# Matrix products between blocks of attention scores, as pairs of 64-row tiles, with a new order on all engines

## What is computed

```python
# one layer; layer 0 also normalizes q and k per head (_ln over the 18 numbers of a head, gains g_q, g_k)
mod = silu(c) @ w_mod + b_mod                       # six vectors of 288 per sample
xn  = _ln(x) * (1 + scale_msa) + shift_msa
q, k, v = split_heads(xn @ w_qkv + b_qkv)           # 16 heads of 18
attn = softmax(einsum('bhqd,bhkd->bhqk', q, k) * 18 ** -0.5)
x = x + gate_msa * (merge_heads(attn @ v) @ w_proj + b_proj)
xn2 = _ln(x) * (1 + scale_mlp) + shift_mlp
x = x + gate_mlp * (gelu(xn2 @ w1 + b1) @ w2 + b2)  # 288 -> 1152 -> 288
```

## Time and profile before

| what | value |
|---|---|
| time, median of 3 runs | 2550.83 us (2548.33 to 2554.66) |
| profiled execution, its span | 2554.1 us |
| PE busy | 2371.3 us (93%), 21219 matmuls |
| PEld busy | 1990.4 us (78%) |
| DVE busy | 1852.2 us (73%) |
| ACT busy | 1626.7 us (64%) |
| POOL busy | 714.5 us (28%) |
| chain that ended last | PE 63%, DVE 11%, DMA 8% |

### The profile page before, as it was taken

How to read it: one execution, slowest core, us unless ns; L and a number is a source line. 1 busy time by engine, 2 the same in 40 slices (tenths; PEclk the granted TensorE clock), 3 DMA queues, 4 the chain that set the end, 5 groups by cost and what they waited for, 6 DMA issues and landing times.

```text
span 2554.1 us, 56620 instructions
## 1 busy us (share of the span) xinstructions
PE 2371.3 (93%) x21219; PEld 1990.4 (78%) x21219; DVE 1852.2 (73%) x3456; ACT 1626.7 (64%) x3049; POOL 714.5 (28%) x938
## 2 busy tenths in 40 slices
PE   5558999999999999999999899999999999999998
PEld 3336878878888888888787788888888888888878
DVE  6357787787788777777677777777777777777764
ACT  3256666676666766767666666666676666666653
POOL 2012332332333233333222122223222222223222
PEclk8788999999999999999999999999999999999999
DMA  4776757756666666666846755566556655565531
GB/s 102 131 174 106 121 116 121 122 112 119 116 118 115 116 120 112 117 118 112 148 85 111 145 97 100 97 113 103 99 99 105 110 96 104 100 113 97 98 67 42
DMA packets 259208, 280.91 MB, mean 110 GB/s; under 512 B 25930, under 2 KB 243212, under 8 KB 258936
## 3 DMA queue, kind: packets, MB, share of 16 engines
q1 hardware_dynamic: 243888, 247.40, 55.8%
q10 hardware_dynamic: 15048, 29.89, 4.5%
HBM read 101.86 MB, written 26.73 MB: 50 GB/s over the span
## 4 chain that ended last, share of the span: by engine, by line
PE 63%; DVE 11%; DMA 8%; issue 5%; SPq 5%; ACT 4%; POOL 3%; DVEq 0%; POOLq 0%; ACTq 0%
PE psum L783 13%; PE psum L873 7%; PE psum_exp L783 7%; PE psum_max L783 7%; DMA attn_k_stack<-attn_qk_hi 5%; PE psum L933 5%; PE psum L935 5%; PE psum L934 5%; PE psum_exp L849 5%; DVE attn_maxima L1105 4%; PE psum_max L862 4%; SPq L1364 4%; DVE attn_qk_centred L1143 3%; PE psum L790 2%; ACT attn_probs L969 1%
## 5 line engine op out<-in xcount | busy, mean ns | idle before, releaser
L969 ACT ACTIVATE attn_probs<-psum_exp 128x1024 f32<-128x1024 f32 x512 | 526.9, 1029 | 391.4 <-PE psum_exp L849 377.6
L1105 DVE TENSOR_REDUCE attn_maxima<-psum_max 128x4 f32<-128x1024 f32 x512 | 620.6, 1212 | 83.0 <-PE psum_max L862 77.4
L1278 POOL TENSOR_TENSOR mlp_x<-mlp_x,mlp_gated 128x288 f32<-128x288 f32 x128 | 103.4, 808 | 1035.4 <-DVE mlp_gated L1122 1035.4
L783 PE MATMUL psum<-attn_ln_split,w_qkv_split 128*128 128x256 f32 (+3 forms) x2240 | 339.2, 297 | 5.1 <-DVE attn_neg_max_lo L1132 3.1
L933 PE MATMUL psum<-mlp_w_fc_hi,mlp_hidden_hi 128*128 128x288 f32 x1152 | 340.9, 296 | 2.9 <-DVE mlp_w_fc_lo L770 2.0
L934 PE MATMUL psum<-mlp_w_fc_lo,mlp_hidden_hi 128*128 128x288 f32 x1152 | 340.5, 296 | 0.0
L935 PE MATMUL psum<-mlp_w_fc_hi,mlp_hidden_lo 128*128 128x288 f32 x1152 | 340.2, 295 | 0.0
L783 PEld LDWEIGHTS psum<-attn_ln_split,w_qkv_split 128*128 128x128 f32 (+3 forms) x2240 | 284.2, 183 | 54.3 <-issue 25.8
L862 PE MATMUL psum_max<-attn_k_stack,attn_q_stack 62*128 62x256 f32 x2048 | 221.1, 294 | 103.6 <-DMA attn_k_stack<-attn_qk_hi 56.0
L873 PE MATMUL psum<-attn_probs,attn_v 128*32 128x256 f32 x4096 | 282.6, 394 | 1.1 <-ACT attn_probs L969 1.1
L849 PE MATMUL psum_exp<-attn_q_stack,attn_k_stack 64*128 64x256 f32 x2048 | 260.5, 332 | 20.9 <-ACT attn_probs L969 10.9
(11 more groups left out here) (170 smaller groups left out, 4222.1 us busy)
## 6 DMA issues: line engine op xcount, KB each, us to landing
attn_q_stack<-attn_qk_hi SPq DMA_DIRECT2D x256, 128.0 KB
attn_k_stack<-attn_qk_hi SPq DMA_DIRECT2D x256, 128.0 KB
attn_o_and_sums<-attn_o_transposed SPq DMA_DIRECT2D x256, 128.0 KB, 5.0
mlp_gate_and_gated_bias<-modulation ACTq DMA_DIRECT2D x64, 288.0 KB, 3.9
attn_qk_squares<-qk_rstd SPq DMA_DIRECT2D x32, 512.0 KB
attn_q_stack<-attn_qk_lo SPq DMA_DIRECT2D x128, 128.0 KB
attn_k_stack<-attn_qk_lo SPq DMA_DIRECT2D x128, 128.0 KB
attn_x<-in_x_dram SPq DMA_DIRECT2D x32, 288.0 KB, 7.6
```

What stands on the lines that cost most here:

```text
L783: mm = q.matmul(to, lhs, rhs, start=(i == 0), stop=(i == 6))
L969: q.activation(probs[r][:], ps_exp[:], ACT.Exp, scale=SCORE_SCALE).then_inc(S["exps"], 1)
L1105: q.tensor_reduce(maxes[g % 2][:, p // QUARTER, :, p % QUARTER, :], ps_max[:].rearrange("p a (t n) -> p a t n", t=TT), AX.X, ALU.max).then ...
L1278: q.tensor_tensor(xt, xt, gated2[:], ALU.add).then_inc(S["added2"], 1)
```

## The change

Three things change together.

First, the products of v, the projection, the MLP and four of the query and key chunks are made two outputs at a time. A pair of outputs (`low`, `high`) goes into two banks. In a first pass one uses the lower 64 rows of each operand and the other the upper 64 rows, as two tiles of 64 rows at once; in a second pass they change places. A wait for the first pass stands ahead of the second, since both write the same bank. Where no block of scores stands between the two passes (`spaced` is false), the products stay whole, 128 rows each.

```diff
+        def lower_and_upper(q, low, high, half, split):
+            for i in range(len(WIDE_PAIRS) if split else 0):
+                done_low = part_matmul(q, low, i, LOWER, i == 0, False)
+                done_high = part_matmul(q, high, i, UPPER, i == 0, False)
+            if split:
+                done_low.then_inc(S[half], 1)
+                done_high.then_inc(S[half], 1)
+                halves[half] = halves.get(half, 0) + 2
+        def upper_and_lower(q, low, high, split):
+            for i in range(len(WIDE_PAIRS)):
+                first, last = not split and i == 0, i == len(WIDE_PAIRS) - 1
+                done_low = part_matmul(q, low, i, UPPER if split else ROWS, first, last)
+                done_high = part_matmul(q, high, i, LOWER if split else ROWS, first, last)
+            return done_low, done_high
...
+                if (g := due(T, V_FIRST)) is not None:
...
+                    lower_and_upper(q, *[v_product(g, t) for t in range(TT)], "v_half", spaced(T, when(V_SECOND, g)))
+                if (g := due(T, V_SECOND)) is not None:
+                    split = spaced(when(V_FIRST, g), T)
+                    if split:
+                        q.wait_ge(S["v_half"], halves["v_half"])
+                    low, high = upper_and_lower(q, *[v_product(g, t) for t in range(TT)], split)
```

```diff
-                    for m in range(CHUNKS):
-                        j, half = divmod(m, 2)
-                        if half == 0:
-                            bank = bank_of(("fc1", g, j))
-                        mm = wide_matmul(q, bank[:, half * N:half * N + N], w1, slice(m * P, m * P + P), acts2, slice(0, N), True)
+                    for m in (0, 4):
+                        products = [fc1_product(g, m + i) for i in range(4)]
...
+                        lower_and_upper(q, products[0], products[1], "fc1_half", True)
...
+                        lower_and_upper(q, products[2], products[3], "fc1_half", True)
+                        for i, pair in enumerate((products[0:2], products[2:4])):
+                            q.wait_ge(S["fc1_half"], CHUNKS // 2 * 2 * g + m + 2 * i + 2)
+                            low, high = upper_and_lower(q, *pair, True)
```

Third, the table of places is new for all engines. Places are now in quarters of a slot (STEP = 4), a step's read-out has a place of its own on each engine, and a dict gives single samples (the first ones, those around the boundary of the layers, the last one) places of their own. Banks are written out in tables instead of being picked. One line of the table before, and what answers to it:

```diff
-VAR_AT = -28
-RSTD_OUT, RSTD_IN = -26, -25
+VAR_AT, RS_AT = (-28.25, -28.25, {B - 1: -29.0}), (-28.25, -28.25, {0: -31.5, B - 1: -29.0})
+RSTD_OUT, RSTD_IN = -28.25, -23.25
```

374 lines of the change are left out of this document (231 added, 143 removed).

## The result

The changed kernel takes 2542.52 us, median of 6 runs (2530.15 to 2544.57), against 2551.26 us before (6 runs, 2548.33 to 2554.66): ratio 0.9954, 95% interval 0.9942 to 0.9966. It is faster, by 9 us where the forecast said 121. Its profiled execution spans 2540.5 us, 13.6 less than before.

The account below looks back on a forecast made before the run. PE's own queue was taken to bound the steady part. The sum 2554.1 - 73 + 10 - 25 - 25 - 10 = 2431 put the median at about 2430 us, with 50% on 2400 to 2465 and a wider range of 2380 to 2500.

Parts of the forecast that it names:

- Pairs at the pace of whole products: PE's products: a pair of 64-row products costs the 0.12 us of one full product, so taken at nothing.
- rival 4: PE's pairs don't keep the scores' pace; above 0.1335 us a pair all gains go, at 0.15 2700 us; chance 6%.
- Changes of shape: PE's tile shape changes fall from 1448 to 1048, at 0.19 or 0.11 us each: -73 us.
- Second halves wait: On PE, second halves wait for first halves' semaphore where only one block of scores lies between: +10 us, 0 to +20.
- Scores spread out: PE's steady waits, 63 us, shrink by 40% as score blocks for the maxima stand further apart: -25 us, 0 to -60.
- First samples: At the start, the landing of the keys' stack falls out of the loop of three samples: -25 us, 0 to -45.
- The boundary: Around the change of layers, own places for the samples there give back PE's idle time: -10 us, 0 to -15.
- rival 2: DVE's in-order queue keeps layer 0 near 37.7 us a sample, only layer 1 gets shorter: median about 2505; chance 7%.
- Rival 1: The order removes no wait; only the 73 us of shape changes come, less 10 for half waits: median 2488; chance 20%.

Follow-up runs that it names:

- the first experiment: Changed kernel's order of all engines, but with whole 128-row products in place of the pairs of half products: 2605.97 us, ratio 1.0194 to the kernel before.
- e14: Changed kernel with the eight chunks of the MLP's first product as whole products one after the other, the rest in pairs: 2555.16 us, ratio 1.0002.
- e2: Changed kernel with layer 1's PSUM banks for the value products and the last two query and key chunks dealt out anew: 2591.01 us, ratio 1.0141.
- e3: Changed kernel with layer 1's first transpose of the maxima one block of scores later on PE: 2541.04 us, ratio 0.9938.
- e4: Changed kernel with the banks of the MLP's first four products swapped, chunks 0 and 1 with 2 and 3: 2561.59 us, ratio 1.0032.
- e12: Changed kernel with the loads of layer 0's MLP weights 4 and 7 slots later on ScalarE's queue: 2540.11 us, ratio 0.9933.
- e16: Changed kernel with layer 1's last MLP chunk in bank 7 and the transposes' second bank 6, exchanging the two: 2537.32 us, ratio 0.9937.
- e18: e16 plus, in layer 1, projection's second halves behind the third probability product (so far 2572.74 us), and first query and key pair later: 2593.62 us, ratio 1.015.

## Why the prediction was wrong

*Pairs at the pace of whole products:* right, 0.120 and 0.132 us; rival 4 never had a case here. The code's DMA grew to 244 packets in 0.8% of the engines' time, and in the steady stretches PE's waits without a named releaser are none in ten samples of layer 0 and 0.8 us in ten of layer 1. The Trainium skill, "TensorEngine Tiling (Array Packing)", section Instruction Overhead, puts about 60 cycles of overhead on each matmul; this trace does not bear that out as a cost to be added: with 9118 more matmuls a pair keeps the 0.120 and 0.132 us of a whole product.

*Changes of shape, -73 us:* right on PE: 1.17 and 1.22 us a sample, and -74 by the same steps over the whole program. *Second halves wait, +10:* right in kind and size. The semaphore itself costs 0.01 us, but the load behind it is uncovered, 0.1 us, at one or two places a sample. It is contained in the waits below.

***Scores spread out, -25:* this is the step that failed.** It took 40% of the 63 us of steady waits away; they grew instead, by 1.08 us a sample in layer 0 and 0.97 in layer 1, +50 us over the 52 samples of the parts above. I had followed one kind of wait, the scores' blocks for the reductions, and it did get better: in layer 1 the one of up to 0.6 us before the maxima is gone. I had not gone along the other round trips in the new order: which bank each product takes and who empties it. Before, banks were dealt to whichever had been free longest; now they are fixed, pairs need two at once, and bank 4 is asked for right behind the probability product that fills it. With whole tiles this makes the order's waits equal to before's; that the rest, 0.9 to 1.2 us, comes with the pairs is shown by the first experiment. For three places of layer 1 the traces show how (a change of shape stood over a round trip, and taking it away bought waiting); with two first loads of second halves they make up 0.77 of 0.91 us. For layer 0 the trace names the waits (the keys' stack, which was not among PE's waits in ten samples before, and the maxima) and the chain through the reciprocals' transfers, 12 us long in the sample shown; that this chain makes the added wait is argued and not shown. I had costed every change as if it were on the path.

*First samples, -25:* measured -6.7, of which some 3.5 are changes of shape. The variance product did go ahead, but the stacks did not land less than 38 us apart: PE's waits for the keys' stack end at 151.1 and 198.2 us. PE's wait for the keys' stacks in 60 to 235 us, before:

```profile
PE psum_max L862 <- DMA attn_k_stack<-attn_qk_hi: 47.6, 4, 17.3
```

and after:

```profile
PE psum_max L950 <- DMA attn_k_stack<-attn_qk_hi: 11.9, 2, 8.3
PE psum L866 <- ACT attn_probs L1102: 8.4, 3, 5.1
PE psum_max L950 <- issue: 8.1, 1, 8.1
PE psum L978 <- DVE attn_maxima L1237: 5.1, 1, 5.1
PE psum_exp L937 <- DMA attn_q_stack<-attn_neg_max_lo: 5.0, 1, 5.0
```

The 8.1 us without a named releaser end at 74.15 us, where before the wait for the first landing ended at 73.97, and are likely the same wait. The other three took the place of the rest, and the first block of scores for the exponentials starts 4.6 us later. The last of the five waits is for a transfer that took 19 us:

```profile
145.83 19.26 DMA attn_q_stack<-attn_neg_max_lo
```

*The boundary, -10:* samples 29 to 35 took 3.6 us more, with 7 us less of changes. Not examined further.

The sum in measured terms, profile against profile: -74 (changes), +50 (steady waits), -3 (first samples without their changes), +10 (boundary without its changes), +3 (the last two samples without theirs): -14, where the spans give -13.6. The nearest rival in time was rival 2 at 2505 us; its picture of layer 0 came, 37.68 us a sample, but not its reason, since lighter reductions help the kernel before as much, and its layer 1, 1.3 us a sample shorter, became 0.2. Rival 1, the order removing no wait, is borne out in its mechanism by the first experiment, and missed at 2488 us because it too kept the full price of the changes. None of the rivals had waits that grow.

Open: which of layer 0's two chains (reciprocals, stacks) would have to be shortened first; one place offers itself, SyncE's queue, where the issue of the reciprocals' read stands behind a wait for the store of x (the 3.69 us of DMA ahead of it in the chain), and it was not tried. Open too is e14, and the boundary.

## What to carry to other kernels

A cost taken off the busiest engine is worth its full price only where nothing else is being waited out at that place. Before one counts changes, walk each round trip (who fills a bank, who empties it, which of the engine's instructions asks for it next) in the new order and see how much work lies over it; a change of shape counts as such work. A table of places is a tuned whole: of seven moves of a few entries (e2, e3, e4, e12, e16 to e18, the last two on top of e16), each against a wait plainly seen in the trace, three gained nothing that can be told from noise, though one of these, e16, did take its wait out, and four cost 19 to 51 us, because the instruction or bank moved held something else.

## What the runs showed of the hardware

Two products of 64 rows that both add to what their banks hold run side by side at the pace of one of 128 rows: 0.120 us a pair at 256 columns, for 6.7 us at a stretch, and 0.132 at 288. A change of tile shape costs 0.19 to 0.21 us where nothing is waited for, and nothing where it stands over a longer wait (two places at bank 4). The first pair behind a wait takes 0.22 us and not 0.12 at 256 columns, even when the tile shape stays. A transfer of 8 KB that found all 16 DMA engines busy (270 GB/s in 145 to 166 us) took 19.3 us to land; moving two loads of weights out of the way did not shorten PE's wait for it (5.0 us, then 5.6), so the crowd as its cause is not shown.
